# Tanh of pairwise sums on ScalarE: Vector adds chosen pairs of units for one 2,048-column tanh, and gathers wait for their own row tile

## What is computed

```python
# layer 2: a shared expert and 2 of 8 routed experts per row
shared = expert(x, Wg_s, Wu_s, Wd_s)          # silu(x Wg^T) * (x Wu^T) Wd^T
scores, idx = top_k(sigmoid(x Wr^T + rb), 2)
out = shared + sum_e cw[e] * expert(x, Wg[e], Wu[e], Wd[e])
# layer 3: every row against the 64 context rows of its batch
txt_proj  = textual_features @ Ws             # (8, 64, 256)
feat_proj = features @ W                      # (8, 512, 256), features = layernorm(x)
h   = tanh(txt_proj[:, None, :, :] + feat_proj[:, :, None, :] + b)   # (8, 512, 64, 256)
rho = einsum('bftd,d->bft', h, w)             # then a masked softmax over t
# ws = tanh(txt_h . Wcw + bcw), bs = tanh(txt_h . Wcb + bcb); layer 3 gives ws * features + bs
# layer 4: layernorm, quantize to int8 steps, ternary weights, bias
```

## Time and profile before

| | before |
|---|---|
| median of 3 runs | 1,129.01 us (1,126.61 to 1,130.82) |
| the profiled execution | 1,128.25 us |
| its span in the profile | 1,126.5 us |
| granted TensorE clock, mean | 0.97 |
| busy: TensorE, ScalarE, Vector, POOL | 1,007.1, 704.4, 664.9, 213.4 us |

### The profile page before, as it was taken

One profiled execution on the slowest core, in us unless ns is written; L12 is line 12 of the kernel. 1 busy time (PEld: TensorE's weight loads), 2 busy tenths in 40 slices (PEclk: granted clock), 3 DMA queues, 4 the chain that ended last, 5 costly groups with the idle time before them and its releaser, 6 DMA issues.

```text
span 1126.5 us, 23210 instructions
## 1 busy us (share of the span) xinstructions
PE 1007.1 (89%) x8772; PEld 768.6 (68%) x8772; DVE 664.9 (59%) x1902; ACT 704.4 (63%) x1154; POOL 213.4 (19%) x257
## 2 busy tenths in 40 slices
PE   6789999999889999999999999999999999948561
PEld 2467777778779998877777777777777777513120
DVE  2567778887723345434276266366366466796746
ACT  1211111111101110699999999999999999999990
POOL 1033212333320003031030030030030030120000
PEclk9969999999989999999999999999999999989995
DMA  8011110111167999766466466466466564010000
GB/s 247 24 61 61 52 40 32 43 38 38 43 239 243 336 335 340 265 228 200 139 231 215 144 223 216 156 211 215 166 202 214 176 197 145 21 33 20 1 20 19
DMA packets 114050, 164.19 MB, mean 146 GB/s; under 512 B 13235, under 2 KB 70068, under 8 KB 113940
## 3 DMA queue, kind: packets, MB, share of 16 engines
q1 hardware_dynamic: 104004, 135.57, 36.3%
q0 software_dynamic: 9936, 27.15, 6.6%
HBM read 138.69 MB, written 23.99 MB: 144 GB/s over the span
## 4 chain that ended last, share of the span: by engine, by line
PE 53%; ACT 27%; DVE 11%; issue 8%; DMA 0%; POOL 0%; SPq 0%; POOLq 0%; DVEq 0%
PE bank L1108 16%; PE bank L1291 9%; PE bank L1270 8%; PE bank L1113 5%; ACT tanhs L644 4%; ACT tanhs L643 4%; ACT arena L643 3%; ACT arena L644 3%; PE bank L1261 3%; ACT shared_w L644 2%; ACT shared_w L643 2%; PE bank L1150 2%; PE bank L1094 2%; PE bank L1165 2%; ACT tanhs L635 2%
## 5 line engine op out<-in xcount | busy, mean ns | idle before, releaser
L1108 PE MATMUL bank<-rowsT,expert_w 128*128 128x128 f32 x2272 | 277.1, 275 | 0.5 <-DVE rowsT L917 0.5
L1108 PEld LDWEIGHTS bank<-rowsT,expert_w 128*128 128x128 f32 x2272 | 270.0, 192 | 7.2 <-issue 3.3
L628 ACT ACTIVATE act<-bank 128x512 f32<-128x512 f32 x103 | 63.5, 616 | 217.3 <-PE bank L1108 112.6
L934 DVE COPY rows_out<-bank 128x256 f32<-128x256 f32 x71 | 30.1, 424 | 192.8 <-PE bank L1270 192.8
L1270 PE MATMUL bank<-expert_w,act 128*128 128x256 f32 x568 | 139.4, 388 | 0.8 <-issue 0.8
L554 POOL DMA_DIRECT2D expert_rows<-rows_out x71 | 40.2, 566 | 511.6 <-DVE rows_out L934 511.0
L643 ACT ACTIVATE tanhs<-arena,txtT 128x512 f32<-128x512 f32 x168 | 128.3, 764 | 4.3 <-DVE arena L960 4.3
L644 ACT ACTIVATE tanhs<-arena,txtT 128x512 f32<-128x512 f32 x168 | 128.3, 764 | 0.0
L1113 PE MATMUL bank<-normT,shared_w 128*128 128x256 f32 x512 | 125.0, 392 | 0.0
L1270 PEld LDWEIGHTS bank<-expert_w,act 128*128 128x128 f32 x568 | 102.3, 190 | 32.7 <-issue 21.7
L643 ACT ACTIVATE arena<-arena,txtT 128x512 f32<-128x512 f32 x144 | 110.0, 764 | 0.0
(11 more groups left out here) (232 smaller groups left out, 1444.0 us busy)
## 6 DMA issues: line engine op xcount, KB each, us to landing
expert_w<-in_WgT SPq DMA_DIRECT2D x71, 512.0 KB, 4.0
expert_w<-in_WuT SPq DMA_DIRECT2D x71, 512.0 KB, 5.2
expert_w<-in_WdT SPq DMA_DIRECT2D x71, 512.0 KB, 6.7
rows_in<-rows_by_expert SPq DMA_DIRECT2D x71, 128.0 KB, 5.4
expert_rows<-rows_out POOLq DMA_DIRECT2D x71, 128.0 KB, 4.3
x<-in_x SPq DMA_DIRECT2D x8, 512.0 KB, 5.5
out<-x SPq DMA_DIRECT2D x16, 256.0 KB, 4.7
score<-in_fside SPq DMA_DIRECT2D x8, 128.0 KB, 2.3
```

Of the source, the lines that this page charges most:

```text
L628: e.activation(act[n % 2][:, :], banks[2 * (n % 2)][:, :], ACT.Tanh, scale=0.5).then_inc(s_tanh, 1)
L1108: got = e.matmul(bank[:, i * P:(i + 1) * P], w[:, at:at + P], t[:, c * P:(c + 1) * P], start=c == 0, stop=c == DC - 1)
```

## The change

1. `added(b, m)` now chooses neighbouring pairs of units, `m` = 2p and 2p + 1. Of the 16 pairs per half, `PAIRS[b]` are chosen, evenly spread, the last of each group always: 2 in batch 0, 4 in batches 1 to 5, 8 in batch 6, 12 in batch 7. Vector adds both units, and at the odd one ScalarE applies one tanh of 2,048 columns to both tiles (`wide_pair`).
2. For this the tiles are laid out in contiguous pairs: `arena` has six instead of five, `normT` becomes one tensor, and `featT` moves from `arena` to the last 1,024 columns of `shared_w` (2048 to 3071), which leaves two tiles there. There are still 16.
3. A gather waits, at each even step, for the stores of the tiles that its own row tile can need: 2(4b + i + 1) + 7 instead of 8(b + 1) + 7.
4. Gathers, adds and the statistics of each row tile make a chain part of their own (`collect`), from `zero` - 71 to `zero` - 27.5 in batch 0 and from 8.5 to 44 places after the previous batch's start in the others; the rest of `mix_in` follows.
5. `feature` of the second half moves from place 3 to 20, `mix_out` from 8.5..52.5 to 8..50.5, `preadd` from 2 to 3 places ahead, `find` from 18 to 0.5 places (batch 0: from -60 to -70), and the lags are new.

```diff
-PLACES = {"attend": 72, "route": 36, "late": -59, "mix_first": -46, "mix_in": 24.5, "mix_in_end": -3, "feature": 3, "sum": 5,
-          "mix_out": 8.5, "mix_out_end": 52.5}
+PLACES = {"attend": 72, "route": 36, "late": -59, "gather_first": -71, "norm_first": -27.5, "gather": 8.5, "norm": 44,
+          "mix_in_end": -3, "feature": 20, "sum": 5, "preadd": 3, "mix_out": 8, "mix_out_end": 50.5}
+PAIRS = {0: 2, 1: 4, 2: 4, 3: 4, 4: 4, 5: 4, 6: 8, 7: 12}
 LAGS = {
-    "sync": {"load_side": -1.5, "narrow": -5},
-    "gpsimd": {},
-    "scalar": {"gate_act": -2.5, "soft_rho": 1, "softmax": -2, "spread": 7.5, "squash": 2, "tanh": 1.5, ("turn", "mix"): -0.5,
-               "turn_e": 1.5},
-    "vector": {"add": 0.5, "add_bias": 1.5, "affine": 0.5, ("aggr", "att"): 2.5, ("aggr", "lin"): -0.5, "choice": -1.5,
-               "convert": -10.5, "find": 3, "gate_act": 3, "linear": 1.5, "narrow": 2, ("newton", "att"): 2, ("newton", "lin"): 2,
...
-    "tensor": {"count": -1.5, "scores": -0.5, "spread": 2.5, "sum": 1, "text": 1.5, ("turn", "mix"): -0.5, "weigh": -2},
+    "sync": {"fetch": -3, "load_side": -1.5, "narrow": -5},
+    "gpsimd": {("power", "lin"): -1, ("power", "moe"): -1},
+    "scalar": {"gate_act": -2.5, "soft_rho": 1, "softmax": -2, "spread": 7.5, "squash": 0.5, "tanh": 1.5, ("turn", "att"): -0.5,
+               ("turn", "mix"): -0.5, "turn_e": 1.5},
+    "vector": {"add": 0.5, "add_bias": 1.5, ("aggr", "att"): 2.5, ("aggr", "lin"): 1, "choice": -1.5, "convert": -20.5, "find": 4.5,
+               "gate_act": 3, "linear": 5, "narrow": 2, ("newton", "att"): 2, ("newton", "lin"): 2, ("newton", "mix"): 1,
+               ("newton", "moe"): 1, "place": -0.5, ("power", "att"): 3, "preadd": -1.5, "quantize": 1, "rho": -2.5, "rsum": 1,
+               ("scale", "mix"): 0.5, ("scale", "moe"): -0.5, "side": -3.5, "soft_rho": -0.5, "softmax": 0.5, ("stats", "att"): 2.5,
+               ("stats", "mix"): 1.5, "step": 2, "sums": 3.5, "text": 10.5, ("turn", "moe"): -0.5, "turn_q": -2, "turn_rows": 1.5,
+               "weigh": -1},
+    "tensor": {"count": -1.5, "feature": -2, "linear": 2.5, "scores": -0.5, "spread": 2.5, "sum": 0.5, "text": 8,
+               ("turn", "mix"): -0.5, "weigh": -2},
 }
...
+    def collect(self, b):
+        steps = []
+        for i in range(self.ST + 1):
+            for j in range(2):
+                steps.append(([("gather", b, 2 * i + j)] if i < self.ST else []) + ([("add", b, 2 * i - 2 + j)] if i else []))
+            if i:
+                steps[-1].append(("stats", "mix", b, i - 1))
+        return steps
...
     def added(self, b, m):
-        return b >= self.B - 2 and m % 2 == 1
+        pairs, share = self.T // 4, int(PAIRS[b])
+        return m // 2 * share // pairs != (m // 2 + 1) * share // pairs
...
-        wide = [tanhs[:, 1024 * i:1024 * (i + 1)] for i in range(6)] + [arena[:, 1024 * i:1024 * (i + 1)] for i in range(5)]
-        wide += [normT[i][:, :] for i in range(2)] + [shared_w[:, 1024 * i:1024 * (i + 1)] for i in range(3)]
+        wide_pair = [tile[:, 2048 * i:2048 * (i + 1)] for tile, n in ((tanhs, 3), (arena, 3), (normTs, 1), (shared_w, 1)) for i in range(n)]
+        wide = [pair[:, 1024 * i:1024 * (i + 1)] for pair in wide_pair for i in range(2)]
-        featT = [arena[:, 5120 + 512 * c:5632 + 512 * c] for c in range(DC)]
+        featT = [shared_w[:, 2048 + 512 * c:2560 + 512 * c] for c in range(DC)]
...
-                    tiles = 2 * ST * (b + 1) + E - 1
+                    tiles = 2 * (ST * b + j // 2 + 1) + E - 1
                     if j == 0:
                         e.wait_ge(s_found, b + 1)
+                    if j % 2 == 0:
                         for r in range(OUTS):
                             e.wait_ge(s_stored[r], 16 * len(range(r, tiles, OUTS)))
...
                     if plan.added(b, m):
-                        e.wait_ge(s_wide_in, wide_in_no[u] + 1)
-                        e.activation(w, w, ACT.Tanh).then_inc(s_wide, 1)
+                        if m % 2:
+                            e.wait_ge(s_wide_in, wide_in_no[u] + 1)
+                            e.activation(wide_pair[u % WIDE // 2], wide_pair[u % WIDE // 2], ACT.Tanh).then_inc(s_wide, 2)
...
-                    e.wait_ge(s_sum, u - WIDE + 1)
+                    if u >= WIDE:
+                        e.wait_ge(s_sum, u - WIDE + 1)
```

44 lines of the change are left out of this document (22 added, 22 removed).

## The result

The change is faster: 1,096.85 us median of 4 runs (1,094.63 to 1,098.02) against 1,129.91 of 4 runs of the kernel before beside them, ratio 0.9709 (95% interval 0.9681 to 0.9737). That is 33 us; I had forecast 14 and a range down to 1,108. The profiled execution took 1,098.02 us with a span of 1,096.3, so 30.2 us of span have to be found.

The account below looks back on a forecast made before the run. TensorE was taken to lead until 461 us, tie with ScalarE until about 961, then ScalarE alone. Savings 7.1 + 1.0 + 4.3 + 2.7 - 0.5 = 14.6 us, 1 held back, gave 1,115 us; range 1,108 to 1,124.

Parts of the forecast that it names:

- TensorE, whose 83 us a batch stay: Batches 0 to 5: TensorE keeps 83 us a batch, hiding ScalarE's 28.6 us saving; only 4.3 us of waits go.
- I cost both at nothing: Later batches' gathers at new places and SP's fetches three places earlier: no cost, 0 us.
- Its waits for tanh are only 4.3 us: TensorE between 476 and 976 us: seven waits for tanh, 4.3 us in all, which the change removes.
- ScalarE's whole saving shows: Rival, all 512 units: ScalarE's 36 us saving shows in full, 1,092 us, if TensorE is shorter than it looks; chance 0.04.
- Price of the long tanh: ScalarE's 2,048-column tanh: 1.80 us start to start, bounds 1.62 and 1.89, against 2.45 for two plain units.
- Behind the last gate product: After tile 70's gate product: ScalarE 7.1 us less, plus its 1.0 us lateness at that gate gone.
- Vector covered: Vector's extra sums in batches 1 to 5 and 7 are covered and cost nothing; upper bound 5 us in batch 7.
- Gathers ahead of tile 22: Earlier gathers of the first batch remove TensorE's stops near 436 us: 2.7 us off, bounds 0 and 1 us loss.
- Tail: From the last tanh's end to the end: same chain, one sum more, plus 0.5 us, a tail of 27.5 us.

Follow-up runs that it names:

- e15: Kernel before with 32 of 512 columns of each plain ScalarE tanh left out in batches 1 to 5: 1,135.72 us in one run, beside 1,134.01.
- e17: e1's kernel run again on another chip, ten runs: 1,137.97 us, ratio 1.0004 to the kernel before.
- e9: Changed kernel with its new order, but units summed and tanh made as before (no pairs): 1,123.03 us, ratio 0.9956 to the kernel before.
- e13: Kernel before with each gather in batches 1 to 5 replaced by a plain one-row DMA: 1,130.24 us in one run.
- e3: Changed kernel with share 2 in all of batches 0 to 5: 1,108.01 us, ratio 0.9768 to the kernel before.
- e1: Kernel before with a quarter of each plain ScalarE tanh left out in batches 1 to 5: 1,107.31 us in one run.
- e7: Changed kernel with all 16 pairs per half in batch 7 instead of 12: ratio 0.9734 to the kernel before.
- e4: Changed kernel with shares 4, 8, 8, 8, 8, 8 in batches 0 to 5: 1,112.89 us, ratio 0.9808 to the kernel before.
- e12: Changed kernel once more, unedited, on another set of runs: ratio 0.9739 to the kernel before.
- e6: Kernel before with only the new gather wait, gathers at their old places: 1,133.97 against 1,134.93 us, ratio 0.9985.
- e14: Kernel before with a quarter of each plain ScalarE tanh left out in batches 1 and 2 alone: 1,133.86 us in one run, beside 1,134.01.
- e16: Kernel before with a tanh cut whose condition never holds, so the kernel before again: 1,135.28 us in one run, beside 1,134.01.
- e18: Kernel before with 128 already satisfied semaphore waits added in TensorE's prologue, shifting its code: 1,137.21 us, ratio 1.0005.
- e10: Kernel before with pairs, long tanh and paired tiles, but old order and old gather wait: 1,106.15 us, ratio 0.9828.

## Why the prediction was wrong, point by point

- **Third part: "TensorE, whose 83 us a batch stay": wrong, and this is 16.1 of the 16.6 us by which the span beat the forecast.** TensorE did need 83.8 us before, and relieving ScalarE alone does nothing while that holds (e15, e17: 499.0 and 500.4 us against 498.3), even less than the 4.3 us that I gave it. But 3.1 us of each batch were the stall, and the changed kernel doesn't have it. Then ScalarE's 82.9 would have been next (e9, e13: 82.3 and 83.0), and the pairs take that away too. ScalarE relieved alone gained nothing in the third part (e15, e17). No stall and no pairs gained 3.4 and 5.9 us there (e13, e9) and lost all or most of it in the last part: -0.2 and 1.0 us are left from tile 22 to the end. Both together gained 20.4 in the third part: down to TensorE's 80.2 us, the floor that e3 and the changed kernel share. The stall is 17.7 us of that; a batch of the old order without it takes 80.7 (e1).
- **The step that failed: "I cost both at nothing",** of the gathers' and fetches' new places. I had asked what the moved gathers do to POOL's queue and to the adds, and not what they had done to TensorE where they stood: 19.6 us of idle weight loads, against 2.4 after. Which of the new order's moves takes the stall away is not isolated; e13 shows only that it needs the gathers.
- **"Its waits for tanh are only 4.3 us": misread.** The earlier trace rows says "issue" and not ScalarE. The loads' row beside it had 19.6 us.
- **The rival "ScalarE's whole saving shows"** (1,092 us, 0.04) was nearer in its time than the forecast. "TensorE to be shorter than it looks" was its condition, and that came true in part: by 3.1 us a batch, and not by the rest of the 5.2 that the rival wants (82.9 to 77.7).
- **Price of the long tanh: right.** 1.80 us from start to start was forecast and measured. Its duration is 1.89 to 1.91 us, what VectorE: DVE Perf Modes, section "The TRN2 errata", of the Trainium skill gives with 224 + 2,048 cycles (1.893). As a cost it would be 0.09 us too much a pair: starts decide, not durations.
- **Behind the last gate product: right.** 8.0 us against 7.6. ScalarE waits for that gate as forecast, and then not again until its last tanh:

```profile
938.34 0.60 ACT L648 ACTIVATE act<-bank 128x512 f32<-128x512 f32 x1 [1.58 <-PE bank L1130]
```

- **Vector covered: right** at share 12 in batch 7 (e7 shows where it ends) and at share 4 in batches 1 to 5 (e4 shows where that ends).
- **Gathers ahead of tile 22: not borne out.** 2.7 us were forecast. The stop near 436 is gone, but a new one of 1.68 us came, since Vector now meets its adds earlier and still waits for the gathered rows (timelines of Vector and TensorE after):

```profile
419.87 0.48 DVE L974 SCALAR_TENSOR_TENSOR x<-picked,share,x 128x256 f32<-128x256 f32 x1 [2.32 <-DMA picked<-expert_rows,found_at]
...
422.56 1.96 PE L1292 MATMUL bank<-expert_w,act 128*128 128x256 f32 x8 [1.68 <-DVE rowsT L938]
```

The part gave 0.8 us in this trace; in e12, the same kernel, it took 3.5 us more than before, with three stops of 4.2 us in all. Two traces of one kernel differ by more than the gain looked for.
- **Tail: right.** From the last tanh's end to the end it is 27.6 us against 27.2.

What stays open: what makes the weight loads slow beside the gathers; which of the new order's moves takes that away; why the old order had the stall on three chips of this study (12 groups each in e6, e14 to e16, e17 and e18) and not in e1 and e10 on a fourth; and whether pairs alone gain anything where it exists. None of the eight runs with the new order and pairs in all batches has it: three on the chip of e6, four on a fifth, and after. Only the three on e6's chip, and after if it ran where before did, count fully, as no old order was traced on the fifth.

## What to carry to other kernels

When two engines both look full, read the weight loads' rows for "issue" and compare one and the same group at several places: where it is half as long again there is a stall, and what else runs at that place is the first suspect. Two limits that stand close, here 83.8 and 82.9 us, hide each other, so that removing either alone shows next to nothing. One run that fits a theory is not enough: e1 bore out a wrong one until it was run again on another chip. And look in the trace for what an edit should have changed: e16's trace shows at once that it changed nothing.
